# Crossed attentions of a fused two-layer kernel: query weights folded into the keys, and the scores turned so that keys lie on the partitions

## The reference, cut to what matters

```python
Q_char = x @ Wq_c.T + bq_c;  K_sub = ctx @ Wk_s.T + bk_s;  V_sub = ctx @ Wv_s.T + bv_s
char2sub = softmax(Q_char @ K_sub.T * scale) @ V_sub            # 2048 queries, 1601 keys
Q_sub = ctx @ Wq_s.T + bq_s; K_char = x @ Wk_c.T + bk_c; V_char = x @ Wv_c.T + bv_c
sub2char = interp_linear(softmax(Q_sub @ K_char.T * scale) @ V_char, 2048)   # 1601 queries, 2048 keys
gate = sigmoid(concat([char2sub, sub2char]) @ Wg.T + bg)
x = x + gate * char2sub + (1 - gate) * sub2char
```

## Time and profile before

| what | us |
|---|---|
| median of 3 runs | 1022.65 (1022.2 to 1022.79) |
| span of the profiled execution | 1021.7 |
| PE busy in it | 988.4 |
| DVE busy | 683.4 |
| ACT busy | 510.3 |
| POOL busy | 401.9 |
| first product of weights and values in the first attention | 580.53 |
| result of the first, last tile of the first attention | 587.6, 754.9 |
| result of the first, last tile of the second attention | 786.0, 1004.0 |

### The profile page before, as it was taken

One profiled execution on the slowest core, in us unless ns is written; L12 is line 12 of the kernel. 1 busy time (PEld: TensorE's weight loads), 2 busy tenths in 40 slices (PEclk: granted clock), 3 DMA queues, 4 the chain that ended last, 5 costly groups with the idle time before them and its releaser, 6 DMA issues. The chain is left out here.

```text
span 1021.7 us, 18534 instructions
## 1 busy us (share of the span) xinstructions
PE 988.4 (97%) x6842; PEld 909.7 (89%) x6842; DVE 683.4 (67%) x1631; ACT 510.3 (50%) x1045; POOL 401.9 (39%) x630
## 2 busy tenths in 40 slices
PE   9999999899999999999999999999999999999995
PEld 8898998688899999987888888899999899999995
DVE  7677777577688888765685555544546676677665
ACT  6356666432477777752445433333335444444442
POOL 4515555516334433415622000000015767767651
PEclk9999999998999999999999999999999999999997
DMA  8200000201688888824214200000001011101000
GB/s 235 83 1 1 1 1 2 82 2 63 199 260 263 252 260 255 259 75 129 67 53 152 45 1 22 1 1 1 1 1 22 16 32 27 32 21 27 22 12 16
DMA packets 57151, 76.52 MB, mean 75 GB/s; under 512 B 5552, under 2 KB 37936, under 8 KB 57072
## 3 DMA queue, kind: packets, MB, share of 16 engines
q1 hardware_dynamic: 40736, 51.61, 16.5%
q0 software_dynamic: 15648, 22.81, 7.7%
q10 hardware_dynamic: 688, 1.05, 0.3%
HBM read 61.43 MB, written 14.02 MB: 74 GB/s over the span
## 5 line engine op out<-in xcount | busy, mean ns | idle before, releaser
L43 PE MATMUL bank<-V_hi,XT_lo 128*128 128x256 f32 x416 | 123.7, 297 | 0.0
L2518 DVE TENSOR_TENSOR XT_lo<-bank,XT_lo 128x512 fp32r<-128x512 f32 x116 | 73.4, 633 | 74.3 <-ACT XT_lo L2175 73.6
L2175 ACT ACTIVATE XT_lo<-bank 128x512 fp32r<-128x512 f32 x116 | 64.0, 553 | 113.6 <-PE bank L1882 112.9
L45 PE MATMUL bank<-V_hi,XT_lo 128*128 128x256 f32 x416 | 117.1, 282 | 0.0
L44 PE MATMUL bank<-V_lo,XT_lo 128*128 128x256 f32 x416 | 116.8, 281 | 0.0
L2523 DVE TENSOR_REDUCE part<-wide 128x1 f32<-128x402 f32 (+1 forms) x116 | 72.3, 624 | 35.5 <-PE wide L45 33.4
L43 PE MATMUL wide<-expert_w_hi,XT_hi 128*128 128x402 f32 (+2 forms) x236 | 92.9, 394 | 1.1 <-DVE XT_hi L2559 0.9
L45 PE MATMUL wide<-expert_w_hi,XT_hi 128*128 128x402 f32 (+2 forms) x236 | 87.1, 369 | 0.0
L44 PE MATMUL wide<-expert_w_lo,XT_hi 128*128 128x402 f32 (+2 forms) x236 | 86.9, 368 | 0.0
L43 PEld LDWEIGHTS bank<-V_hi,XT_lo 128*128 128x128 f32 x416 | 78.3, 188 | 3.5 <-DVE XT_lo L2518 1.7
L44 PEld LDWEIGHTS bank<-V_lo,XT_lo 128*128 128x128 f32 x416 | 78.9, 190 | 0.4
(11 more groups left out here) (503 smaller groups left out, 3279.8 us busy)
## 6 DMA issues: line engine op xcount, KB each, us to landing
sraw<-w1T SPq DMA_DIRECT2D x14, 512.0 KB, 5.3
sraw<-w3T SPq DMA_DIRECT2D x14, 512.0 KB, 6.2
sraw<-w2T SPq DMA_DIRECT2D x14, 512.0 KB, 6.5
raw_even<-w1T SPq DMA_DIRECT2D x11, 512.0 KB
raw_even<-w3T SPq DMA_DIRECT2D x11, 512.0 KB
raw_even<-w2T SPq DMA_DIRECT2D x11, 512.0 KB, 5.4
XT_hi<-queries POOLq DMA_DIRECT2D x16, 256.0 KB, 3.2
routed_results<-rys POOLq DMA_DIRECT2D x15, 256.0 KB
```

The source lines that it names most:

```text
L43: pe.matmul(out, wh, xh, start=first, stop=False)
L45: return pe.matmul(out, wl, xh, start=False, stop=last)
L2175: act.activation(weights(g, nk, 0), transposed(g, nk), ACT.Copy).then_inc(sem["high"], 1)
L2518: dve.tensor_tensor(weights(g, nk, 1), transposed(g, nk), weights(g, nk, 0).bitcast(F32), ALU.subtract).then_inc(sem["low"], 1)
```

## The change

Three things are changed, all in the third block.

1. **Query weights folded into the keys'.** Q·K = x Wq^T Wk ctx^T + terms of the biases. `fold` multiplies the two weights once for each attention (30 products), together with the bias columns. Keys are projected with the product, the raw transposed context or tokens serve as queries. The term that depends on the key alone (t_s, t_c) is an extra column of the value projection and is added as a bias per key. Query projections and the way of the queries through DRAM go.
2. **Scores turned.** A block is two key tiles (stationary) by two query tiles (moving, 256 columns): a key lies on a partition, the queries along the row. The first attention has 5 groups of 2 query tiles with 8 blocks each and one group of 3 query tiles (322 columns) with 16 blocks of one key tile, the second 8 groups of 2 with 7 blocks each (the last of one key tile): 112 blocks. The transposes of the weights go, since the exponentials come out with keys on the partitions, as `weighted` wants them. The maximum of a query now lies across partitions: ACT copies the scores to SBUF with the key term as bias (`evacuate`), DVE keeps a running maximum (`maximum`), at a group's end PE turns it (`max_turn`), DVE reduces it (`tops`), ACT spreads it (`spread_max`), PE turns it back (`spread_turn`), and DVE subtracts it from every block (`subtract`) before ACT takes the exponential in place. `high` and `low` split it as before.
3. **Sums from a column of ones.** The high part of the values has two more columns that hold 1, so the row sum comes out of `weighted`; DVE reads it in `finish`.

Two banks hold scores (before: four), a ring of three holds the split exponentials. The tokens leave SBUF and come back tile by tile, and SP stores a result before it fetches the token tile three further on. The per-token rest is now laid on the seven blocks of a pair of tiles: u is the even, v the odd tile of the pair before the current group.

The diff, cut to its core. The three loops over n stand in the blocks of PE, ACT and DVE in this order; n is the block, b its number in its group:

```diff
@@ closing_expert, PE and after it ACT @@
+                            if b == NB - 1 and c == 2:
+                                pe.wait_ge(t_low, 4)
+                                fold(pe, wk, wq, bk, turning, next_low, 2, fold_done)
...
+                    folded_weight()
                     hi(NB - 1, FC - 1)
@@ cross_phase @@
+            SG, CG = 6, 8
+            GROUPS = [(2 * g, 2 if g < SG - 1 else 3) for g in range(SG)] + [(2 * q, 2) for q in range(CG)]
...
+                    def score(n):
+                        g = group_of[n]
+                        w, x = width(g), slice(GROUPS[g][0] * P, GROUPS[g][0] * P + width(g))
+                        q_hi, q_lo = (XT_hi, XT_lo) if in_cross(g) else (CT_hi, CT_lo)
+                        if n >= 2:
+                            pe.wait_ge(evacuated, n - 1)
...
+                    def weighted(n):
...
+                        for j, k in enumerate(keys_of(n)):
+                            for t in range(GROUPS[g][1]):
+                                if opens(n) and j == 0 and g:
+                                    pe.wait_ge(finished, tiles_before[g - 1] + min(t + 1, GROUPS[g - 1][1]))
+                                x = slice(j * w + t * P, j * w + t * P + chunk(g, t))
+                                dst = weighted_bank[t][0:chunk(g, t), :]
+                                pe.matmul(dst[:, 0:D + 2], hi[:, x], v_hi(k), start=opens(n) and j == 0, stop=False)
+                                pe.matmul(dst[:, 0:D], hi[:, x], v_lo(k), start=False, stop=False)
+                                m = pe.matmul(dst[:, 0:D + 2], lo[:, x], v_hi(k), start=False, stop=closes(n) and k == keys_of(n)[-1])
...
                     def turn(i):
+                        pe.wait_ge(finished, NC + i + 1)
+                        pe.wait_ge(copied, i + 1)
...
                     def x_turn(i):
                         pe.wait_ge(normal, i + 1)
+                        if 0 < i < LAST:
+                            pe.wait_ge(out_done, i)
...
+                    for n in range(NBLK):
+                        b, u, v = post(n)
+                        weighted(n)
+                        if real(u) and b == 0:
+                            turn(u)
+                        if real(u) and b == 1:
+                            gate(u)
+                        if real(v) and b == 2:
+                            interpolate(v)
+                        if real(v) and b == 3:
+                            turn(v)
+                        if real(v) and b == 4:
+                            gate(v)
...
+                        for m in behind[n]:
+                            score(m)
...
+                        if real(u) and b == 3:
+                            x_turn(u)
...
+                        if real(v) and b == 6:
+                            x_turn(v)
...
+                    for n in range(NBLK):
+                        b, u, v = post(n)
+                        for m in range(n, n + 4):
+                            if sub_end[n] <= m < sub_end[n + 1]:
+                                exponent(m)
+                            if high_end[n] <= m < high_end[n + 1]:
+                                high(m)
...
+                        if real(u) and b == 2:
+                            squash(u)
+                        if real(v) and b == 3:
+                            copy(v)
...
+                        for m in behind[n]:
+                            evacuate(m)
...
+                    for n in range(NBLK):
+                        b, u, v = post(n)
+                        for m in range(sub_end[n], sub_end[n + 1]):
+                            subtract(m)
+                        if real(u) and b == 2:
+                            move(u, 0)
+                            move(u, 1)
...
+                        for m in range(high_end[n], high_end[n + 1]):
+                            low(m)
...
+                        if real(u - 1) and b == 2:
+                            for k in range(2, 8):
+                                softly(u - 1, k)
+                            add(u - 1, 0)
+                            add(u - 1, 1)
...
+                        if real(u) and b == 6:
+                            for k in range(2, 8):
+                                softly(u, k)
+                            add(u, 0)
+                            add(u, 1)
...
+                        for m in behind[n]:
+                            maximum(m)
```

More of the change, by code:

```diff
@@ L1822, in _ @@
+                    for i in range(NT):
+                        sp.wait_ge(out_done, i + 1)
+                        sp.dma_start(out[0, i * P:(i + 1) * P, :], token(i)).then_inc(stored, 16)
+                        sp.wait_ge(stored, 16 * (i + 1))
+                        if i + 3 < NT:
+                            token_back(i + 3)
                 @blk.tensor
@@ new lines, in evacuate @@
+                    def evacuate(n):
+                        g = group_of[n]
+                        w = width(g)
+                        act.wait_ge(scored, n + 1)
+                        if place_free(n) > 0:
+                            act.wait_ge(low_done, place_free(n))
+                        if 11 <= n < 14:
+                            act.wait_ge(fold_low, n - 10)
+                        if n < first[1]:
+                            act.wait_ge(unit_low, 1 + max(UNITS.index(("v", k, 0)) for k in keys_of(n)))
+                        if g >= SG + 2 and g % 2 == 0:
+                            act.wait_ge(rows_split, NC)
+                        if g == SG:
+                            act.wait_ge(unit_low, NV + sum(k not in EARLY for k in range(keys_of(n)[-1] + 1)))
+                        for j, k in enumerate(keys_of(n)):
+                            m = act.activation(place(n)[:, j * w:(j + 1) * w], score_bank[n % 2][:, j * w:(j + 1) * w], ACT.Identity,
+                                               bias=(t_c if in_cross(g) else t_s)[:, k:k + 1])
+                        m.then_inc(evacuated, 1)
@@ new lines, in spread_max, with exponent @@
+                    def spread_max(g):
+                        act.wait_ge(topped, g + 1)
+                        if g:
+                            act.wait_ge(spread_turned, g)
+                        for t in range(GROUPS[g][1]):
+                            n = chunk(g, t)
+                            m = act.activation(spread_out[t][0:n, :], ident[0:n, :], ACT.Identity, bias=top[0:n, t:t + 1], scale=0.0)
+                        m.then_inc(spread, 1)
+                    def exponent(n):
+                        act.wait_ge(lowered, n + 1)
+                        act.activation(place(n), place(n), ACT.Exp, scale=scale).then_inc(exped, 1)
@@ L2516, in low @@
-                    def low(i, g, sem, nk):
-                        dve.wait_ge(sem["high"], i * G + g + 1)
-                        dve.tensor_tensor(weights(g, nk, 1), transposed(g, nk), weights(g, nk, 0).bitcast(F32),
-                                          ALU.subtract).then_inc(sem["low"], 1)
-                    def maximum(i, g, sem, n):
-                        dve.wait_ge(sem["scored"], i * G + g + 1)
-                        dve.reduce_max(part[:, g:g + 1], in_wide(g, n), AX).then_inc(sem["chain"], 1)
@@ L2651, in _ @@
                         dve.bn_aggr(out=MV[:, 2 * i:2 * i + 2], in_=stats[:, 6 * i:6 * i + 6]).then_inc(stat3, 1)
-                    dve.wait_ge(S_["chain"], 1)
-                    for u in range(2, 8):
+                    for u in range(2, 7):
                         unit(u)
@@ L2656, in _ @@
                     token_low(1)
[L2657 removed]
+                    for u in range(7, 14):
                         unit(u)
[L2659 to L2665 removed]
```

1384 lines of the change are left out of this document (674 added, 710 removed).

## The result

The changed kernel takes 1102.15 us in the median of 4 runs (1095.96 to 1102.73), the kernel before 1022.42 (1022.03 to 1022.79), 79.7 us more. The profiled execution is one of the 1102.15 us, with a span of 1100.3.

What follows compares the result with a forecast made beforehand. TensorE bounds the kernel before; in the changed one the order of waits does. First pair of the second attention at 791, plus 246, 28 for the end, 21 for the clock: 1086.5, with 0.95 about 1088 us; range 1030 to 1125.

Steps and rivals of the forecast that it cites:

- 8 x 2.86: First attention: TensorE work of a pair's eight steady blocks, each 24 products of 0.119 us, that is 2.86 us.
- -52 us: Whole kernel: TensorE work taken off (weight transposes, query products) less work put on (scores, folds, turns of maxima).
- the rival of the hidden waits: Whole kernel: queued work covers the waits and TensorE still sets the pace, about 985 us; chance 0.13.
- Start and first attention: First weights-values product at 580 us, five pairs in 134, three-tile group 47.8, second attention's first pair at 791.
- the ring: Each steady block: subtract, exponent, evacuate twice, maximum and hops between VectorE and ScalarE take 2.7 us (2.6 to 3.2).
- The sign of 25 to 27 us a pair: First attention: pairs of query tiles 25 to 27 us apart would show the prediction right.
- Second attention: Eight pairs take 246 us by the order of waits, full groups 38.0 each; falls of the clock add 21.
- the wait for `add`: Second attention: the odd tile's x_turn waits for the even tile's add, TensorE idle 5.9 us a pair.
- the one for `copy`: Second attention: the odd tile's turn waits for copy, queued behind exponent on ScalarE, TensorE idle 4.6 us a pair.
- The end: After the last result: last tile's chain 17.7 us, plus 4.8 for tile 13 and 5.5 for tile 14, 28 together.
- the main case: Whole kernel: waits in the queues' order plus falls of the clock give 1088 us, range 1075 to 1104; chance 0.45.
- it would stay low for most of a group: Second attention: seven groups with 5 us more at half pace; rival shared with slower blocks, 1105 to 1130 us, chance 0.16.

Runs made afterwards that it cites:

- the better order: Own bank for odd tiles, copy and normalise before the exponential, finish before low; here on the changed kernel without its maximum: 991.81 us, ratio 0.9696.
- `copy`: Changed kernel with the odd tile's copy queued on ScalarE ahead of the block's exponential instead of behind it: 1086.88 us, ratio 1.0640.
- filled: Changed kernel with 32 and 44 unused products added ahead of the odd tile's turn and x_turn: 1085.21 us, ratio 1.0632.
- own bank: Changed kernel with the per-token products of odd tiles in a bank of their own: 1084.21 us, ratio 1.0625.

## Why the prediction was right

1. **The work taken off TensorE.** The 8 x 2.86 of a pair of the first attention was measured where nothing else held it up (23.2 us a pair without the maximum). The -52 us are about right too: in the last kernel built on the changed one, with no maximum and the better order, TensorE is busy for 932.7 us; with the estimated 6.4 for the turns of the maximum put back that is 939, 49 less than the 988.4 before. That 52 us of work bring nothing by themselves when the waits move in is what the rival of the hidden waits denied; it fell (985 forecast, 1102 measured).
2. **Start and first attention.** The first product of weights and values was forecast at 580 and started at 579.53. The fifth pair was forecast at 714 and came at 720.4, the first pair of the second attention at 791 and came at 799.0. Two things make up most of these 8 us. The smaller is the ring. It was put at 2.7 us and measures 2.85:

```profile
645.70 0.68 DVE L2680 TENSOR_TENSOR Fx<-Fx,bank 128x512 f32<-128x512 f32 x1
...
646.42 0.63 ACT L2345 ACTIVATE Fx<-Fx 128x512 f32<-128x512 f32 x1 [0.84 <-DVE Fx L2680]
...
647.08 0.84 ACT L2330 ACTIVATE Fx<-wide,t_s 128x256 f32<-128x256 f32 x2
...
647.95 0.69 DVE L2659 TENSOR_TENSOR rows<-rows,Fx 128x512 f32<-128x512 f32 x1 [0.96 <-ACT Fx L2330]
...
648.55 0.68 DVE L2680 TENSOR_TENSOR sraw<-sraw,bank 128x512 f32<-128x512 f32 x1
```

`subtract` 645.70, `exponent` 646.42, `evacuate` 647.08, `maximum` 647.95, next `subtract` 648.55: the exponential in place takes 0.63 before the next step can start, not the 0.51 taken from a start to the next; only its latency of the earlier trace rows was near. That leaves no slack against TensorE's 2.86. The larger is the clock, for which I had counted no fall here: it was granted 0.95 from 580 to 720 us. Four kernels have the same code up to here, and their four intervals from the first pair to the fifth, forecast at 106.5 us, go with the clock granted: 111.8 (the changed kernel) and 111.7 (`copy`) at 0.95, 108.9 (filled) at 0.98, 107.4 (own bank) at 0.99. So some 4 us come and go from one execution to the next, and about 1 is left for the ring. The sign of 25 to 27 us a pair was therefore missed in this execution (27.8, 28.0, 26.5, and 29.5 for the fifth). This may also be why one run of the changed kernel took 1095.96 (its clock over the whole run was 0.954, that of the others 0.948); it has no trace to show it.
3. **Second attention.** 267 us were forecast from the first pair to the last (246 and 21 for the clock), 269.3 came (799.0 to 1068.3). Full groups: 38.0 + 3.0 forecast, 41.0 measured; the filled kernel puts the clock's part at 2.5. That the sum is met to the tenth is luck in part: the wait for `add` was put 0.5 too short and the one for `copy` 0.7 too long, the clock 0.5 too high and the rest as much too low. The path is not luck. Both waits are where they were said to be, ended by the instructions named, and each went when its cause was taken away.
4. **The end.** 28 us forecast, 1100.3 - 1068.3 = 32.0 measured. I had kept the last tile's chain of before, 17.7 us, and added two to it, 10.3 us; 14.3 came. The low clock of the end is not the whole answer: TensorE was granted 0.71 here, but 0.68 before as well, where the 17.7 were measured. Before, then after:

```profile
1004.00:1021.70 17.70, 7.57 (x36) 5.67 (x36) 7.85 (x29) 3.93 (x12) 3.11 (x7) 0.68 0.07 24
```

```profile
1068.00:1100.30 32.30, 15.31 (x78) 13.44 (x78) 16.20 (x56) 7.33 (x20) 5.20 (x12) 0.71 0.06 21
```

TensorE is busy for 7.7 us more than in the end before, so the half clock can account for a part of the 4 us missed, not shown how large; the end was about as long, 30.6 to 32.3 us, in every variant, also where order and maximum were mended.
5. **The sum.** 1086.5 on the span against 1100.3, 13.8 short: some 8 until the first pair of the second attention, 2 in it, 4 at the end. The measured 1102 lies in the main case's range, near its top. Of the rivals, the clock as a mechanism was right and is in the sum; that it would stay low for most of a group was wrong, it was back about 4 us after work had begun again, as the windows at 904 and 924 show. The Trainium skill, "TensorE: Matmul & The Clock Gate", HAM oscillation, describes a kernel that falls back in each step because it waits between bursts of products. The trace agrees: 0.86 with the waits, 1.00 with them filled.

What stays open: why the clock falls in the first attention in one execution and not in another, and the 4 us put on the fold in the closing expert, which was not run alone (only the start at 579.53, which holds it, was met). Nor was the folding of the weights run without the turned scores, and the 4 us of the end are not divided.

## What to carry to other kernels

A layout that takes work off the bound engine can lose if it turns a reduction along a row into one across partitions: price the whole ring that this adds to the other queues (here a copy, a maximum, a subtraction and the hops between them in each block), not their busy shares. In a kernel of in-order queues, follow one period through all of them by hand and list every wait whose releaser stands behind a long stretch; that gave 41 us a pair before the kernel ran. And a wait of TensorE has a second price, the half clock after it.

## What the runs showed of the hardware

Some 530 products whose results nobody uses, put into the waits, brought the grant of the second attention from 0.86 to 1.00 and made the kernel 17 us faster, 3 of them in the first attention, where nothing was changed. A wait of 3.9 us showed in the grant only after work had begun again (1.00 in the window at 899, 0.89 at 900, 0.50 at 901), and the low grant lasted a little over 3 us; in a wait of 6.1 us the grant fell during the wait (0.93 at 917, 0.50 at 918) and was at 0.66 in the window at 924. An exponential of 128x512 in place in SBUF took 0.63 us, a subtraction with an operand in PSUM broadcast over two key tiles 0.68, no more than the plain one from PSUM (0.69).
